# Splitting attention queries and keys into two float32r parts, with two heads in the two halves of TensorE's rows

## The reference

```python
q = layernorm(x) @ Wq + bq          # 512 x 256, 16 heads of 16
k, v = ctx @ Wk + bk, ctx @ Wv + bv # 1024 x 256
s = q_h @ k_h.T / sqrt(16)          # 512 x 1024 for each of 16 heads
s = where(mask, s, -1e30)           # block 1 alone
x = x + g * (softmax(s) @ v_h) @ Wo
```

## Time and profile before

| | us |
|---|---|
| median of 3 runs | 5177.25 (5173.41 to 5180.86) |
| span of the profiled execution | 5182.7 |
| of it the first part, with the units' scores | about 0 to 2250 |
| PE busy / DVE / ACT / POOL | 4823.6 / 3429.4 / 3112.6 / 2409.7 |

### The profile page before, as it was taken

The page is one execution under the profiler, slowest core; times in us unless marked ns, Lnnn a source line. Parts: engine busy times, 40 slices in busy tenths (PEclk is TensorE's granted clock), DMA queues, the critical chain, the costliest instruction groups (busy, mean ns, idle before and its releaser), DMA issues.

```text
span 5182.7 us, 92467 instructions
## 1 busy us (share of the span) xinstructions
PE 4823.6 (93%) x35414; PEld 3013.7 (58%) x35480; DVE 3429.4 (66%) x6514; ACT 3112.6 (60%) x6618; POOL 2409.7 (46%) x2314
## 2 busy tenths in 40 slices
PE   6898999989899898969999999999999999999998
PEld 2232333334334343227877777777777777777776
DVE  4766566676675857757766666666666666666664
ACT  3565555434344444547777677776777677777763
POOL 3211101111011111129777677676767677776762
PEclk8999999999999899989999999999999999999998
DMA  5233222322312222311000000000000000000000
GB/s 121 52 56 59 54 44 55 65 50 48 61 37 50 46 57 43 56 30 46 8 18 26 16 24 20 22 22 20 22 18 24 18 28 16 24 19 19 24 22 21
DMA packets 125161, 188.97 MB, mean 36 GB/s; under 512 B 18896, under 2 KB 67664, under 8 KB 124496
## 3 DMA queue, kind: packets, MB, share of 16 engines
q1 hardware_dynamic: 124720, 183.06, 15.9%
HBM read 150.09 MB, written 32.51 MB: 35 GB/s over the span
## 4 chain that ended last, share of the span: by engine, by line
PE 64%; DVE 14%; ACT 8%; POOL 7%; issue 6%; DMA 1%; SPq 0%; DVEq 0%; POOLq 0%; ACTq 0%
PE psum L1253 16%; PE psum L1300 10%; PE psum L467 4%; PE psum L432 4%; PE psum L453 4%; DVE maxes L655 3%; PE psum L1308 3%; PE psum L1341 3%; PE psum L1332 2%; PE psum L414 2%; PE psum L1323 2%; POOL stats L1633 2%; PE psum L476 2%; ACT probs L836 2%; PE psum L422 1%
## 5 line engine op out<-in xcount | busy, mean ns | idle before, releaser
L836 ACT ACTIVATE probs<-psum 128x1024 f32<-128x1024 f32 x768 | 772.2, 1019 | 609.9 <-PE psum L453 337.7
L655 DVE TENSOR_REDUCE maxes<-psum 128x1 f32<-128x1024 f32 x512 | 616.5, 1212 | 246.6 <-PE psum L432 242.5
L1633 POOL TENSOR_TENSOR stats<-stats,minus_half 128x8 f32<-128x8 f32 x384 | 651.8, 1697 | 32.0
L1439 DVE TENSOR_TENSOR lwork<-psum,rotary 128x512 f32<-128x512 f32 x384 | 264.2, 688 | 513.1 <-PE psum L1300 446.9
L1573 ACT ACTIVATE lprobs<-psum,small_stats,stats 128x128 f32<-128x128 f32 x1536 | 581.1, 474 | 12.3 <-DVE small_stats L1457 11.5
L1629 POOL TENSOR_TENSOR lwork<-lwork 128x512 f32<-128x512 f32 x384 | 493.9, 1286 | 202.9 <-DVE lwork L1441 202.7
L1300 PE MATMUL psum<-wqkv_hi,xs_hi 128*128 128x512 f32 (+1 forms) x1536 | 554.6, 361 | 33.6 <-POOL xs_lo L1620 17.1
L453 PE MATMUL psum<-stack 98*128 98x512 bf16 x1536 | 513.1, 390 | 72.1 <-DVE maxes L655 32.0
L432 PE MATMUL psum<-stack 96*128 96x512 bf16 x1536 | 473.2, 391 | 64.2 <-ACT probs L836 53.1
L1300 PE MATMUL psum<-wqkv_hi,xs_lo 128*128 128x512 f32 (+1 forms) x1536 | 519.6, 338 | 0.0
L1300 PE MATMUL psum<-wqkv_lo,xs_hi 128*128 128x512 f32 (+1 forms) x1536 | 519.3, 338 | 0.0
(11 more groups left out here) (225 smaller groups left out, 11526.7 us busy)
## 6 DMA issues: line engine op xcount, KB each, us to landing
stack<-k_parts SPq DMA_DIRECT2D x288, 128.0 KB
staged<-in_quads SPq DMA_DIRECT2D x144, 256.0 KB, 3.0
k_parts<-parts SPq DMA_DIRECT2D x48, 384.0 KB, 2.9
stack<-q_parts SPq DMA_DIRECT2D x288, 64.0 KB
staged<-in_w SPq DMA_DIRECT2D x54, 256.0 KB, 2.7
ctx<-in_ctxT SPq DMA_DIRECT2D x24, 512.0 KB, 4.7
q_parts<-parts SPq DMA_DIRECT2D x24, 384.0 KB, 2.3
arena<-in_ctxT SPq DMA_DIRECT2D x8, 512.0 KB, 4.8
```

The costliest lines, as they stand in the source:

```text
L655: ins = vector.tensor_reduce(to, pair(("M", u)), AX.XY, ALU.max)
L836: scalar.activation(probs[:, i % 6, :, :], pair(("E", u)), ACT.Exp).then_inc(S_["E_act"], 1)
L1439: vector.tensor_tensor(v4(t1), v4(qk), bc(rotary[:, d % 2, 0, tt], 2, 4), ALU.mult)
L1633: pool_step(gpsimd.tensor_tensor(st[:, 8:16], st[:, 0:8], minus_half[:, :], ALU.pow))
```

## The change

- The parts are now two in float32r (a 32-bit format), and three products of parts are stacked: 48 rows per head. `pk` is gone: ACT L830 and POOL L951 with it, and each write to DRAM holds two parts of 4 bytes in place of three of 2.
- Even heads lie on rows 0 to 47 of the stacks, odd heads on rows 64 to 111. The two products of `E` take the two halves and the two banks of a pair. So do those of `M` in layers 0 and 3: each computes 128 queries by 512 keys for two heads, where before it computed 1024 keys for one. In layer 1 the two products of `M` remain the two key halves of one head, on the same rows. The masks of `E` in layer 1 now come after both scores.
- DVE's maximum writes two columns per `M` in layers 0 and 3. A new step `sha` joins the halves there (one DVE operation on 16 columns), once per group.
- The shifts go to two places: four transfers per group in place of two. The ones are set once by POOL in each of the three buffers (three memsets of 2048 columns) and no longer loaded.
- One buffer less for the output weights; the loads `L1_o` and `L3_o` stand two units later and wait for the last `wo` of the layer before.

```diff
-PAIRS = [(0, 0), (0, 1), (0, 2), (1, 0), (1, 1), (2, 0)]
+PAIRS = [(0, 0), (0, 1), (1, 0)]
 STACK = len(PAIRS) * HD
+HALF_ROWS = P // 2
...
-            if L == 1:
-                put(t + 16, ("sha", (L, b, g)))
+            put(t + 16, ("sha", (L, b, g)))
             put(t + 17, ("sh", (L, b, g)))
...
-    loads = {2: [("wl", "L1_o")], 6: [("wl", "L3_o")]}
+    loads = {4: [("wl", "L1_o")], 8: [("wl", "L3_o")]}
...
-        parts = psb("parts", [P, 3, 3, S], BF16)
-        stacks = [psb(f"stack{i}", [P, 3 * S2]) for i in range(3)]
+        parts = psb("parts", [P, 3, 2, S], F32R)
+        stacks = [psb(f"stack{i}", [P, 3 * S2], F32R) for i in range(3)]
...
+        def head_rows(e, n):
+            return slice(e * HALF_ROWS, e * HALF_ROWS + n)
...
                     for i in range(2):
-                        ins = tensor.matmul(ps[:, i, :], q[0:STACK, h, qt * P:(qt + 1) * P], k[0:STACK, h, i * S:(i + 1) * S],
+                        e, j, half = (h % 2, h // 2, i) if L == 1 else (i, h // 2, h % 2)
+                        on = head_rows(e, STACK)
+                        ins = tensor.matmul(ps[:, i, :], q[on, j, qt * P:(qt + 1) * P], k[on, j, half * S:(half + 1) * S],
                                             start=True, stop=True)
...
                     for i in range(2):
-                        h = 2 * p + i
-                        ins = tensor.matmul(ps[:, i, :], ky[0:STACK + 2, h, kt * P:(kt + 1) * P], q[0:STACK + 2, h, :],
-                                            start=True, stop=L != 1)
-                        if L == 1:
+                        on = head_rows(i, STACK + 2)
+                        ins = tensor.matmul(ps[:, i, :], ky[on, p, kt * P:(kt + 1) * P], q[on, p, :], start=True, stop=L != 1)
+                    if L == 1:
+                        for i in range(2):
                             ins = tensor.matmul(ps[:, i, :], ident_b[:, :], masks_k[:, kt * S:(kt + 1) * S], start=False, stop=True)
...
-                        ins = vector.tensor_reduce(to, pair(("M", u)), AX.XY, ALU.max)
+                        at0 = h % 2 * 16 + h // 2 * QT + qt
+                        ins = vector.tensor_reduce(maxes[:, n % 4, at0:at0 + 9:8], pair(("M", u)), AX.X, ALU.max)
...
+                    if u[0] != 1:
+                        vector.tensor_tensor(mx[:, 0:16], mx[:, 0:16], mx[:, 16:32], ALU.max).then_inc(S_["sha_dve"], 1)
+                        continue
...
-                elif stage == "pk":
-                    i = at_("pj", u) - 1
-                    A.wait_ge(S_["pj_pool"], at_("pj", u))
-                    scalar.activation(parts[:, i % 3, 1, :], buf(("f", u)), ACT.Copy).then_inc(S_["pk_act"], 1)
...
+            gpsimd.memset(kst[n].bitcast(F32), 1.0).then_inc(S_["ones_set"], 1)
...
-                    for i in range(2):
-                        dst = qst[n % 3][STACK + i:STACK + i + 1, :, :].rearrange("r h (t q) -> r (h t) q", q=P)
-                        sync.dma_start(dst, shifts[:, n % 4, i, :]).then_inc(shift_in[n % 4], 16)
+                    for e in range(2):
+                        for i in range(2):
+                            r = e * HALF_ROWS + STACK + i
+                            dst = qst[n % 3][r:r + 1, :, :].rearrange("r j (t q) -> r (j t) q", q=P)
+                            sync.dma_start(dst.bitcast(F32), shifts[8 * e:8 * e + 8, n % 4, i, :].bitcast(F32)).then_inc(shift_in[n % 4], 16)
```

More of the change, by code:

```diff
@@ L274, in first_part @@
         maxes = psb("maxes", [P, 4, 48])
-        shifts = psb("shifts", [16, 4, 2, P], BF16)
+        shifts = psb("shifts", [16, 4, 2, P], F32R)
         masks_q = psb("mask_by_query", [P, QT * S2], BF16)
@@ L283, in first_part @@
         added = psb("added", [P, S])
[L284 to L285 removed]
+        q_dram = {u: nc.dram_tensor(f"q_parts{u[0]}{u[1]}", [D, 2, S], F32).ap() for u in UNITS}
+        k_dram = {u: nc.dram_tensor(f"k_parts{u[0]}{u[1]}", [D, 2, S2], F32).ap() for u in UNITS}
         w_ff = arena[:, 0:4096]
@@ L333, in work_closes @@
             stage, u = p
-            names = {"ln2": [(("ln", u, i), "ln2_pe") for i in range(2)], "pk": [(("f", u), "pk_pool")],
+            names = {"ln2": [(("ln", u, i), "ln2_pe") for i in range(2)], "pj": [(("f", u), "pj_pool")],
                      "r3": [(("sg", u), "r3_dve")]}
@@ L436, in tensor_program @@
                     n = group_of[u]
-                    if u[0] == 1:
-                        PE.wait_ge(S_["sha_dve"], at_("sha", u))
-                    else:
-                        PE.wait_ge(S_["M_dve"], at_("M", u + (3, 3)))
+                    PE.wait_ge(S_["sha_dve"], at_("sha", u))
                     left(one, ("sh", u), PE)
@@ L475, in tensor_program @@
                     for g in range(G4):
-                        ins = tensor.matmul(bank(("wo", u)), wo[L][:, g, m * P:(m + 1) * P], outs[:, g, :], start=g == 0, stop=g == G4 - 1)
+                        ins = tensor.matmul(bank(("wo", u)), wo[:, g, m * P:(m + 1) * P], outs[:, g, :], start=g == 0, stop=g == G4 - 1)
                     ins.then_inc(S_["wo_pe"], 1)
@@ L674, in vector_program @@
                     step.join()
-                    vector.scalar_tensor_tensor(out=shifts[:, n % 4, 1, :], in0=ps, scalar=-1.0, in1=shifts[:, n % 4, 0, :],
+                    vector.scalar_tensor_tensor(out=shifts[:, n % 4, 1, :], in0=ps, scalar=-1.0, in1=shifts[:, n % 4, 0, :].bitcast(F32),
                                                 op0=ALU.mult, op1=ALU.subtract).then_inc(S_["sh_dve"], 1)
@@ L1821, in lay_out @@
     bf16 = i["L1_ffn_kernel"].dtype
-    a["ones"] = np.ones((2, 4 * S2), bf16)
     n, h = S, LHD // 2
```

60 lines of the change are left out of this document (30 added, 30 removed).

## The result

The changed kernel takes 5273.93 us (median; 5246.68 to 5290.96), the kernel before took 5178.91 beside it: a ratio of 1.0178, 95% interval 1.0145 to 1.0211. It is **slower** by 95 us, where 18 us faster was forecast, and lies outside the range of 5085 to 5235. The interval lies wholly above 1, so it is slower; whether by 2% stays unclear.

The account below looks back on a forecast made before the run. It took a loop of PE products, exponential and three pairs of banks as the bound, not PE alone; -54 - 13 + 11 + 29 + 8 + 1 = -18 us against 5182.7 gave 5165, median 5159, range 5085 to 5235.

Parts of the forecast that it names:

- term 5: Layer 1: a turn takes 1.34 us of PE instead of 1.31, over 256 turns; +8 us, bounds -43 and +30.
- Term 3: Changes of the array's division around blocks of whole-array products: 32 us, a third of it on the path; +11 us.
- Term 1: `M` and `E` pairs in layers 0 and 3 run at once on two halves; -54 us, bounds 0 and -106.
- Term 2: Second rounding on ACT gone between projection and exponential, 25 x 0.52 us in layers 0 and 3; -13, bounds 0 and -30.
- Term 4: Two more shift transfers to issue per group, 24 groups x 1.2 us in layers 0 and 3; +29, bounds +10 and +45.
- The clock rival: Less PE work lowers the granted clock in layers 0 and 3 to 0.88: +60 us, hence 5219; chance 0.28.
- That the halves do not run at once: Rival: a pair of half-array products takes 0.47 us for 0.45; 5275 us at worst; chance 0.07.
- That PE was the bound after all: Rival: pairs gain their full -106 us in layers 0 and 3, shifts cost +10; 5088 us; chance 0.15.

Follow-up runs that it names:

- e1: Changed kernel with layer 1's two mask products ahead of the score pair of `E` instead of behind it: 5239.7 us, ratio 1.0113 to the kernel before.
- e3: Changed kernel with layer 1's two `M` products on the two halves of the rows, as in layers 0 and 3: 5230.2 us, ratio 1.0103.
- b4: Kernel before with the `M` pairs of layers 0 and 3 on the first 48 of 96 rows, in bfloat16: 5256.9 us, ratio 1.0160.
- b2: Kernel before with layer 1's `M` pair on the first 48 of 96 rows, in bfloat16: 5215.0 us, ratio 1.0067.
- b1: Kernel before with only the first product of each `M` and `E` pair in layers 0 and 3, except the first group: 5137.3 us, ratio 0.9923.
- e2: Changed kernel with each group's shifts written by two transfers, each to both halves, in place of four: 5250.8 us, ratio 1.0136 to the kernel before.
- e4: Changed kernel with every `M` pair in layers 0 and 3 computed twice into the same banks: 5292.6 us, ratio 1.0226 to the kernel before.
- e5: Changed kernel with both products of each pair in layers 0 and 3 on the first half of the rows: 5551.7 us, ratio 1.0730.

## Why the prediction was wrong, point by point

Two steps failed: term 5, the turn of layer 1, and the clock, for which the sum has nothing although a rival had its price.

- **Term 5, layer 1 (+8, bounds -43 and +30): measured +75. This step failed.** 50 of the 75 us lie at full clock in both kernels, where a turn takes 0.23 us more and +0.03 was forecast. The masks up to `M` were right: 0.43 and one change of 0.1 were put there, and 0.54 was measured. The other two parts were mis-sized, by 0.1 each. The pair of `E` was put at 0.24 up to the masks, with a change 0.34, and takes 0.43. The pair of `M` was put at 0.47, its two products 0.235 apart, and the second starts 0.336 behind the first: 0.31 for the first product after a wait was in the earlier trace rows, but the text took the streaming rate for a pair that in every turn stands behind a change. e1 and e3 show that the order and the halves decide: with both, 81 of the 928 us are gone. The returns from projections, 0.09 each, were not counted either, and 24 us more lie where the clock had fallen in the changed kernel alone.
- **The clock in layers 0 and 3 (nothing in the sum): +61. This step failed too.** Terms 1 to 4 give -54 - 13 + 11 + 29 = -27 us for these layers. Where both kernels have the full clock the change did gain, 25 us. Where the changed kernel alone had lost the full clock, it is 61 us longer. With the small rest that is the measured +35.
- **Term 3, changes in layers 0 and 3 (+11): price, count and share came near, at full clock.** Beside projections and other whole-array products there are 369 such changes in layers 0 and 3 of the changed kernel, about what 20 blocks a unit with two each make (320). At 0.09 us they are 33 us. In b4 some 0.4 of such pauses reached the end at full clock, where a third was taken; what the term lacks is that the clock fell with them. The rule that the Trainium skill states in "TensorEngine Tiling (Array Packing)", Tiling Modes, that a change of mode drains the engine, fits halves of the rows too: no row of before had shown a cost there, b2 does, with its 0.09 us.
- **Term 1, pairs at once (-54): right in kind.** b1 gets 45 us from saved products alone, and DVE's maxima take over as the text said. But most pairs have their follower 0.33 to 0.43 us behind them, not 0.24, which the text itself had named as a sign against it only from 0.45 on. Turns alone went from 3.25 to 3.10 us (3.0 forecast).
- **Term 2, `pk` gone (-13):** two turns with projections take 4.78 us (441.10 to 445.88) for 5.20: 0.42 saved instead of 0.52, with what the pairs save among it. L830 is gone. How much of the 0.42 is its own, no run shows.
- **Term 4, shifts (+29, bounds +10 and +45):** held. Taking the two transfers away gives 23, adding them to the kernel before costs 22. (The term found 1.4 us a group and multiplied 1.2.)
- **Together, layers 0 and 3** without the two added transfers (e2) take 1339 us for 1343: 41 us gained where both have the full clock, 46 lost where it had fallen in e2 alone.
- **The rivals.** The clock rival's condition came true: 0.87 and 0.88, under its 0.93, and so did its size in these layers, 61 us for its 60. Without layer 1's 75 us the kernel would stand at 5199, 20 from its 5219. Its cause, less true work of PE in the same time, fits b1 and e4; b4 and e5 add that the clock also falls with PE's records as full as before or fuller, and a busy PE is not PE at its peak. That the halves do not run at once (5275) came out at the measured time by luck, for a cause that is not there: they start 3 to 4 ns apart, and on one half (e5) the time is 278 us more. That PE was the bound after all was given 0.15, at a time of 5088. For layer 1 at full clock it holds on the side of what is added: b2's 35 us of pauses cost 44, 29 of them at full clock. For what is taken away it does not: b1's 225 us give 45.
- **DVE** still takes 1.93 us in turns with inverted sums, as forecast:

```profile
2203.76 1.17 DVE L662 TENSOR_REDUCE maxes<-psum 128x2 f32<-128x1024 f32 x1
...
2205.69 1.17 DVE L662 TENSOR_REDUCE maxes<-psum 128x2 f32<-128x1024 f32 x1
```

What stays open is what made the clock fall. The pauses of the changes and of the shifts (b4, e2) each go with it, and no run holds the clock still.

## What to carry to other kernels

When a change puts products on a part of the array, write PE's order for one whole turn, mark each place where the division changes (whole array, halves of the rows, strips of columns), and price both sides of each, here 0.09 us; a side where the division changed before costs nothing new. Where PE sets the pace, as in layer 1, that is time on the path; where other engines do, look at the clock as well: 61 us of layers 0 and 3 and 24 of layer 1 lay where it had fallen. Then order the products so that those of one division stand together, and do not leave two float32r products behind each other on the same rows where they can go to different ones. With these two edits and the transfers put together the time went from 1.8% over that of before to 0.6% under it, in a kernel whose layer 1 subtracts maxima that are not each head's own. What was saved on PE here was worth less than what was added to it cost: 45 of 225 us in b1, 83 for 68 in b4, and in both the clock fell.

## What the runs showed of the hardware that had not been expected

- A change between a product on 48 rows and one on 98 or 128 rows adds 0.09 us to the start of what follows, also with bfloat16 throughout (b2: 0.312 for 0.218 us). Where the next product is in 32-column strips nothing is added (b2: 0.306 for 0.307).
- Two float32r products of 512 columns on the same half of the rows start 0.335 us apart behind a change of division or a wait, and 0.235 directly behind another such pair (e1, e5); on two halves 3 to 4 ns apart.
- The granted clock does not follow PE's busy share: 0.95 at 549 of 621 us busy (before), 0.92 at 469 of 593 (b1), 0.87 at 545 of 641 (after), 0.92 at 576 of 642 (e4), 0.90 at 608 of 664 (b4), 0.76 at 732 of 770 (e5). In b4, with pauses between the products, and in e5, with the same products one after the other, it was lower than in the kernel that each was made from; in e4, with more products in the same time, it was higher. A busy record can hold a pause, so these shares are not PE's work.
